# A state-space block's second pass: the sums over states moved from VectorE to ScalarE and accumulating DMAs, with four decay buffers

## The reference

```python
x = x + 0.5 * ffn(layernorm(x))            # ternary weights, bias
x = x + mamba(layernorm(x))
x = x + 0.5 * ffn(layernorm(x))

# inside mamba, per token t, with 16 states n for each of 1024 features d:
dA  = exp(dt[t, d] * A[d, n])              # the decay
dBu = dt[t, d] * B[t, n] * u[t, d]
h   = dA * h + dBu                         # a scan over the 4096 tokens
y[t, d] = sum_n h[d, n] * C[t, n]          # the sum over 16 states
y = (y + u * Dskip) * silu(z);  out = y @ W_out.T
```

## Time and profile before

| what | value |
|---|---|
| median of 3 runs | 3009.37 us (3003.62 to 3009.72) |
| the profiled execution's own time | 2999.02 us |
| its span, first to last instruction | 2997.2 us |
| mean granted TensorE clock | 0.911 of full speed |
| DVE busy | 2510.7 us, 84% of the span |
| PE busy | 2453.4 us, 82% |
| ACT busy | 1956.5 us, 65% |
| POOL busy | 1919.4 us, 64% |

### The profile page before, as it was taken

How to read it: one execution, slowest core, us unless ns; L and a number is a source line. 1 busy time by engine, 2 the same in 40 slices (tenths; PEclk the granted TensorE clock), 3 DMA queues, 4 the chain that set the end, 5 groups by cost and what they waited for, 6 DMA issues and landing times.

```text
span 2997.2 us, 42932 instructions
## 1 busy us (share of the span) xinstructions
PE 2453.4 (82%) x12448; PEld 1406.8 (47%) x12448; DVE 2510.7 (84%) x3325; ACT 1956.5 (65%) x3464; POOL 1919.4 (64%) x1705
## 2 busy tenths in 40 slices
PE   3678898889888736788888888888888888898897
PEld 1333344344343314555555555555555555555553
DVE  5566766767766639999999999999999999999991
ACT  2234756765755756677777777777767776777772
POOL 1112222222221128899989989989989989999993
PEclk8688999999998857899999999999999998999999
DMA  5554323323232245352353342352352352443331
GB/s 198 182 197 148 113 100 128 106 100 134 83 123 106 78 161 164 96 130 72 99 132 82 99 132 77 100 135 71 106 131 76 104 121 82 108 112 94 105 71 42
DMA packets 175914, 337.14 MB, mean 112 GB/s; under 512 B 42721, under 2 KB 92129, under 8 KB 175393
## 3 DMA queue, kind: packets, MB, share of 16 engines
q1 hardware_dynamic: 161824, 283.71, 28.3%
q0 software_dynamic: 13824, 50.34, 8.8%
HBM read 174.09 MB, written 109.58 MB: 95 GB/s over the span
## 4 chain that ended last, share of the span: by engine, by line
POOL 24%; DVE 16%; issue 13%; PE 4%; DMA 3%; ACT 1%; POOLq 1%; DVEq 0%; SPq 0%; ACTq 0%
POOL dbu L1051 19%; DVE h L1275 11%; DVE y L1288 4%; DMA y<-y_part 1%; PE p_g L1407 1%; DMA dtu_<-dtu_scratch 1%; PE p_g L1398 1%; PE p_ht L1364 1%; POOL o L1096 1%; POOL y L1071 1%; POOL carry L1062 1%; POOL x L1090 1%; POOL dbu L1056 1%; POOL y L1086 1%; DMA dt_<-dt_scratch 1%
## 5 line engine op out<-in xcount | busy, mean ns | idle before, releaser
L1275 DVE TENSOR_TENSOR_SCAN h<-p_da,dbu 128x512 f32<-128x512 f32 x1024 | 1188.3, 1205 | 42.6 <-ACT p_da L1157 21.8
L1051 POOL TENSOR_TENSOR dbu<-dtu_,bb 128x1024 f32<-128x1024 f32 x512 | 1203.9, 2380 | 4.6 <-DMA dtu_<-dtu_scratch 4.0
L1157 ACT ACTIVATE p_da<-dt_,neg_a 128x255 f32<-128x255 f32 x2048 | 885.6, 467 | 396.4 <-DVE h L1275 376.0
L1364 PE MATMUL p_ht<-ident,h 128*128 128x128 f32 x4096 | 595.2, 305 | 151.7 <-DVE h L1275 150.3
L1364 PEld LDWEIGHTS p_ht<-ident,h 128*128 128x128 f32 x4096 | 533.5, 159 | 242.6 <-issue 106.6
L1288 DVE SCALAR_TENSOR_TENSOR y<-p_ht,ct,y 128x1024 f32<-128x1024 f32 x400 | 505.5, 1264 | 3.1 <-PE p_ht L1364 3.0
L359 POOL TENSOR_TENSOR late<-dt,u 128x512 f32<-128x512 f32 x64 | 82.3, 1286 | 425.6 <-DVE dt L552 425.6
L1398 PE MATMUL p_g<-wo,tokt 128*128 128x512 f16 x1536 | 352.5, 387 | 1.6 <-ACT tokt L1189 1.6
L710 PE MATMUL p_u<-xz,wu 128*128 128x512 f16 x1536 | 350.0, 385 | 0.0
L1407 PE MATMUL p_g<-wz,xz 128*128 128x512 f16 x1536 | 345.7, 382 | 0.0
L70 POOL TENSOR_TENSOR small<-small,consts 128x1 f32<-128x1 f32 x96 | 70.4, 733 | 404.3 <-DVE small L63 404.3
(11 more groups left out here) (121 smaller groups left out, 3082.0 us busy)
## 6 DMA issues: line engine op xcount, KB each, us to landing
y<-y_part POOLq DMA_DIRECT2D x96, 512.0 KB, 5.8
bb<-b_scratch SPq DMA_DIRECT2D x128, 256.0 KB, 3.5
xin<-in_x SPq DMA_DIRECT2D x32, 512.0 KB, 4.3
x_scratch<-x SPq DMA_DIRECT2D x32, 512.0 KB, 3.3
xz_scratch<-xz SPq DMA_DIRECT2D x16, 1024.0 KB, 6.4
y_scratch<-late SPq DMA_DIRECT2D x32, 512.0 KB, 2.9
dt_scratch<-dt SPq DMA_DIRECT2D x64, 256.0 KB, 2.2
dtu_scratch<-late SPq DMA_DIRECT2D x64, 256.0 KB, 2.5
```

The costliest lines, as they stand in the source:

```text
L1051: nc.gpsimd.tensor_tensor(state[:, 4 * f:4 * f + 4, :], dtu[:, 4 * f:4 * f + 4, :], bb[n // NB % 2][:, n % NB:n % NB + 1, :].to_broadcast( ...
L1157: ins_ = nc.scalar.activation(p_da[p % 2][:, k * T2 + 1:(k + 1) * T2], dt[:, g, 1:], ACT.Exp, scale=neg_a[:, g, n:n + 1])
L1275: nc.vector.tensor_tensor_scan(h[n % 2][:, 2 * p:2 * p + 2, :].rearrange("p g t -> p (g t)"), p_da[p % 2][:], dbu[n % 2][:, 2 * p:2 * p + ...
L1364: mm = nc.tensor.transpose(p_ht[t][:, g * P:(g + 1) * P], h[n % 2][:, g, t * P:(t + 1) * P], ident[:])
```

## The change

1. For t = 1, fifteen states (1 to 15) are now multiplied by ACT; DVE adds only state 0. State 2 goes straight into the single tile `y2`; the other fourteen go through one of three `part` tiles and an accumulating DMA each, in two chains: the odd ones into y itself, the even ones into `y2`. `merge` is an accumulating DMA of y2 into y as well, and stands in the odd chain ahead of state 15. The small POOL instruction ahead of each DMA is gone. Each DMA of a chain waits on POOL until the one before it in the chain has landed.
2. The half bias is added to x1 by an accumulating DMA from a copy in DRAM, which the first pass writes once; and the last sum is one DVE instruction, o = p_g * scale + x1, in place of ACT's L1211 and POOL's L1096.
3. The decays have four buffers, one for each pair: the two PSUM banks for pairs 0 and 1, and two new SBUF tiles `s_da` for pairs 2 and 3.
4. Both passes are written out: no hardware loop is left.
5. The gate of t = 1, the mean and the scale that follow it move one step later, some stores and `add_bias` move earlier.

```diff
-            for j in range(TT1):
-                step(1, 1, j, True, True, True)
-            with eng.Fori(0, (C1 - 4) // 2) as turn:
-                for o in range(2):
-                    for j in range(TT1):
-                        step(turn * 2 + 2 + o, o, j, True, True, True)
-            for j in range(TT1):
-                step(C1 - 2, C1 % 2, j, True, True, True)
+            for i in range(1, C1 - 1):
+                for j in range(TT1):
+                    step(i, i % 2, j, True, True, True)
...
+                    if isinstance(k, int) and k == 2:
+                        sp.wait_ge(const_done, 1)
+                        sp.dma_start(dram["hb"], half_bias[:]).then_inc(hb_stored, 16)
...
+        s_da = [sb(f"s_da{i}", [P, HALF]) for i in range(2)]
...
-        y2 = [sb(f"y2_{i}", [P, D]) for i in range(2)]
-        part = [sb(f"y2_part{i}", [P, D]) for i in range(2)]
+        y2 = sb("y2", [P, D])
+        part = [sb(f"y_part{i}", [P, D]) for i in range(3)]
...
-        p_da = banks("p_da", 2)
+        da = [t[:] for t in banks("p_da", 2) + s_da]
...
-        PARTED = (0, 5, 7, 8, 10, 11, 12)
-        SUMS = len(PARTED) - 1
+        PARTED = tuple(range(1, NS))
+        Y2_FIRST, MERGE = 2, NS
+        Y_SUM, Y2_SUM = (1, 3, 5, 7, 9, 11, 13, MERGE, 15), (4, 6, 8, 10, 12, 14)
+        SUMMED = tuple(n for n in PARTED if n != Y2_FIRST)
+
+        def summed(c, n):
+
+            if n in Y_SUM:
+                return y_summed[c % 2], (c // 2 * len(Y_SUM) + Y_SUM.index(n) + 1) * 16
+            return y2_summed, (c * len(Y2_SUM) + Y2_SUM.index(n) + 1) * 16
+
+        def part_of(c, n):
+
+            return c * len(SUMMED) + SUMMED.index(n)
...
-            body(0, 0)
-            body(1, 1)
-            with eng.Fori(0, (C2 - 4) // 2) as turn:
-                body(turn * 2 + 2, 0)
-                body(turn * 2 + 3, 1)
-            for i in range(C2 - 2, C2 + 2):
+            for i in range(C2 + 2):
                 body(i, i % 2)
...
-                    wait_alone(sp, y_added[1], (c - 1) * NS)
+                    for t in range(TT2):
+                        wait(sp, y_added[t], (c - 1) * NS)
...
-                        if e_on and n in (1, 6, 7):
-                            store(i - 2, *{1: (0, 1), 6: (1, 0), 7: (1, 1)}[n])
+                        if e_on and n in (1, 2, 3):
+                            store(i - 2, *{1: (0, 1), 2: (1, 0), 3: (1, 1)}[n])
...
-                def add_part(c, cpar, k):
-                    wait(pool, y_added[1], c * NS + PARTED[k] + 1)
-                    wait(pool, part_added, (c * SUMS + k - 1) * 16)
-                    nc.gpsimd.tensor_tensor(small[:, 44:45], consts["minus_half"], consts["minus_half"], ALU.mult
-                                            ).then_inc(part_ready, 1)
-                    pool.wait_ge(part_ready, 1)
-                    pool.dma_start(y2[cpar][:], part[k % 2][:], accum_op=ALU.add).then_inc(part_added, 16)
+                def add_part(c, cpar, n):
+                    into, sums, done = (y[cpar][1], Y_SUM, y_summed[cpar]) if n in Y_SUM else (y2, Y2_SUM, y2_summed)
+                    wait(pool, y_added[1], c * NS + n + 1)
+                    if sums.index(n):
+                        wait(pool, *summed(c, sums[sums.index(n) - 1]))
+                    pool.dma_start(into[:], part[part_of(c, n) % 3][:], accum_op=ALU.add).then_inc(done, 16)
 
                 def merge(c, cpar):
-                    wait(pool, y_added[1], c * NS + NS)
-                    wait(pool, part_added, (c + 1) * SUMS * 16)
-                    nc.gpsimd.tensor_tensor(y[cpar][1][:], y[cpar][1][:], y2[cpar][:], ALU.add).then_inc(merged, 1)
+                    wait(pool, *summed(c, Y2_SUM[-1]))
+                    wait(pool, *summed(c, Y_SUM[Y_SUM.index(MERGE) - 1]))
+                    pool.dma_start(y[cpar][1][:], y2[:], accum_op=ALU.add).then_inc(y_summed[cpar], 16)
 
                 def gate(c, cpar, t):
                     wait(pool, y_added[t], c * NS + NS)
                     if t:
-                        wait(pool, merged, c + 1)
+                        wait(pool, *summed(c, Y_SUM[-1]))
...
-                    nc.gpsimd.tensor_tensor(x1[t][:], x1[t][:], half_bias[:], ALU.add).then_inc(xb_done, 1)
-
-                def finish(i, c, t, x):
-                    b, m = place(i, "f", t, x)
-                    wait(pool, g_free[b], m + 1)
-                    wait(pool, xb_done, c * TT2 + t + 1)
-                    nc.gpsimd.tensor_tensor(o[x][:], o[x][:], x1[t][:, x * HALF:(x + 1) * HALF], ALU.add).then_inc(fin_done, 1)
+                    pool.dma_start(x1[t][:], dram["hb"], accum_op=ALU.add).then_inc(xb_done[t], 16)
 
...
-                            if n - 3 in PARTED[1:]:
-                                add_part(i, par, PARTED.index(n - 3))
-                        if e_on:
-                            if n == 1:
-                                finish(i - 1, i - 2, 0, 1)
-                            if n == 5:
-                                add_bias(i - 2, 1)
-                            if n in (6, 7):
-                                finish(i, i - 2, 1, n - 6)
+                            if n - 3 in SUMMED:
+                                add_part(i, par, n - 3)
+                        if e_on and n == 0:
+                            add_bias(i - 2, 1)
                         if c_on:
-                            if n == 3:
+                            if n in (0, 1, 3):
+                                add_part(i - 1, 1 - par, {0: 13, 1: 14, 3: 15}[n])
+                            if n in (2, 5):
+                                gate(i - 1, 1 - par, n // 5)
+                            if n == 2:
                                 merge(i - 1, 1 - par)
-                            if n in (2, 4):
-                                gate(i - 1, 1 - par, n // 4)
                             if n in (10, 13):
                                 row_scale(pool, nc, vn, consts["minus_half"], sn, stats_ready, pow_done, scale_ready,
                                           xn_done, (i - 1) * TT2 + n // 13)
                             if n == 12:
-                                if isinstance(i, int) and i == 1:
-                                    pool.wait_ge(bias_done, 1)
                                 add_bias(i - 1, 0)
-                            if n == 15:
-                                finish(i, i - 1, 0, 0)
...
-                        wait(act, scan_done, i * (NS * 4) + n * 4 + p - 1)
+                        wait(act, scan_done, i * (NS * 4) + n * 4 + p - 3)
                         for k in range(2):
                             g = 2 * p + k
-                            ins_ = nc.scalar.activation(p_da[p % 2][:, k * T2 + 1:(k + 1) * T2], dt[:, g, 1:], ACT.Exp,
+                            ins_ = nc.scalar.activation(da[p][:, k * T2 + 1:(k + 1) * T2], dt[:, g, 1:], ACT.Exp,
...
                 def part_state(i, par, n):
-                    k = PARTED.index(n)
                     if n == PARTED[0]:
                         wait(act, ct_loaded[par], (i - par) * 8 + 16)
-                        wait(act, merged, i - 1)
+                    if n == Y2_FIRST:
+                        into = y2
+                        if i:
+                            wait(act, *summed(i - 1, MERGE))
                     else:
-                        wait(act, part_added, (i * SUMS + k - 2) * 16)
+                        k = part_of(i, n)
+                        into = part[k % 3]
+                        if k >= 3:
+                            wait(act, *summed((k - 3) // len(SUMMED), SUMMED[(k - 3) % len(SUMMED)]))
                     wait(act, ht_full[1], i * NS + n + 1)
-                    nc.scalar.activation((part[k % 2] if k else y2[par])[:], p_ht[1][:], ACT.Copy, scale=ct[par][:, 1, n:n + 1]
+                    nc.scalar.activation(into[:], p_ht[1][:], ACT.Copy, scale=ct[par][:, 1, n:n + 1]
...
-                        if e_on and n in (1, 2):
-                            ffn_out(i, i - 2, 1, n - 1)
-                        if c_on and n in (14, 15):
-                            ffn_out(i, c, 0, n - 14)
...
+                        if c_on and n == 0:
+                            part_state(i - 1, 1 - par, NS - 1)
                         if c_on:
-                            if n in (2, 4):
-                                mean_abs(i, c, 1 - par, n // 4)
-                            if n in (3, 5):
-                                scale_y(c, 1 - par, n // 5)
+                            if n in (2, 5):
+                                mean_abs(i, c, 1 - par, n // 5)
+                            if n in (3, 6):
+                                scale_y(c, 1 - par, n // 6)
...
-                        nc.vector.tensor_tensor_scan(h[n % 2][:, 2 * p:2 * p + 2, :].rearrange("p g t -> p (g t)"), p_da[p % 2][:],
+                        nc.vector.tensor_tensor_scan(h[n % 2][:, 2 * p:2 * p + 2, :].rearrange("p g t -> p (g t)"), da[p],
```

(45 more changed lines are left out.)

11 lines of the change are left out of this document (4 added, 7 removed).

## The result

The changed kernel takes 3211.5 us in the median (3207.31 to 3214.15), the kernel before 3008.61: the ratio is 1.0675, with a 95% interval of 1.0658 to 1.0692. It is slower by 203 us; 312 were forecast.

What follows compares the result with a forecast made beforehand. DVE was taken to bound the second pass. A chunk of 132 us with turn-taking, against 112.5, times 16 chunks gave +312 us: 3311 profiled, 3321 us in the median, range 3050 to 3490 (about 8 in 10).

Steps and rivals of the forecast that it cites:

- The bound and the lengths: Second pass: DVE bounds it, busy 109.4 of 112.5 us a chunk; POOL needs 105.5 us of its own.
- The four decay buffers: Scans of pairs 2 and 3, both inputs in SBUF, take full turns with POOL's SBUF readers; chance 77%.
- the 132 us a chunk: Forecast chunk time with turn-taking in the second pass, between 125.3 (no overlap) and 138.7 (POOL delayed by every such scan).
- the walk of the plain step: One second-pass step followed through: third scan waits 1.3 us for POOL's products; 7.4 us a step in place of 7.03.
- The least that wasn't: Claim that SBUF scans (37.1 us) and POOL's SBUF readers (88.2 us) cannot overlap, so a chunk takes at least 125.3 us.
- A reading of the step: Earlier trace: while POOL's two products run, to 1633.95, DVE does two scans, a sum, two scans, overlapping freely.
- Sums moved off DVE: Eight sums leave DVE (9.4 us a chunk), the final sum comes (2.9): 102.9 us busy, 106.0 with 3.1 idle.
- Rival (a): The scan does not contend, or POOL and DVE pass each other: 106 us a chunk, 2905 us median; chance 13%.
- The expected marks: `s_da` scans well above 1.2 us, `p_da` scans at 1.2, POOL's products about 3 us, chunk 125 to 139 us.
- POOL: POOL loses 13.7 us a chunk of work and gains 9.8 of DMA issues: 101.6 us in place of 105.5.
- DMAs and waits: 17 accumulating DMAs a chunk in place of 6; their landings are met, merge included: nothing taken.
- The written-out passes: Loop-turn waits go, 0 to 28.7 us, not taken off the forecast; the first pass put at nothing.

Runs made afterwards that it cites:

- e1: Changed kernel with its decays back in two PSUM buffers, ACT waiting for the scan two pairs before: 2977.1 us, 0.9902 of the kernel before.
- e2: Changed kernel with only pair 3's decay in one SBUF buffer, the other pairs in PSUM: 3073.7 us, 1.0222 of the kernel before.
- e3: Changed kernel with the decays of all four pairs in two alternating SBUF buffers: 3804.4 us, 1.2645 of the kernel before.
- e7: Kernel before with one of its two decay buffers (pairs 1 and 3) in SBUF, half bias tile 512 wide: 3425.6 us, ratio 1.1392.
- e12: Changed kernel with decay buffers exchanged: pairs 0 and 1 read from SBUF, pairs 2 and 3 from PSUM: 3446.1 us, 1.1446 of the kernel before.
- e6: Changed kernel with DVE's final sum of the first token tile's second half moved ahead of the state sum of n = 15: 3170.6 us, ratio 1.0541.
- e8: Kernel before with both passes written out, nothing else changed: 2979.8 us, 0.9908 of the kernel before.
- e5: As e1, with DVE's final sum of the first token tile's second half ahead of the state sum of n = 15: 2962.4 us, ratio 0.9857.
- e9: As e5, with ACT's copies of the low halves behind the decays of pairs 0 and 1: 2937.4 us, 0.9761 of the kernel before.
- e11: As e5, with each of the fourteen accumulating DMAs a chunk moving 8 of 1024 columns: 2956.8 us, 0.9826 of the kernel before.

## Why the prediction was right, and where it was off

**The bound and the lengths.** DVE bound the second pass and still does, its waits for the port counted with it. The DVE work was right: 102.9 us a chunk were forecast without contention; e1's stretch gives 186.04/200 x 111.6 = 103.8.

**The four decay buffers.** The step that decided was right: two SBUF inputs make a scan take turns with POOL's SBUF readers. The first pass's L631 and L521 carried over to the scan. e1, e2, e3, e7 and e12 show it: no scan above 1.23 us without such inputs, and more time with each pair that has them. The rule of the Trainium skill (page "SBUF — State Buffer", section "Who interferes with whom"), by which a VectorE instruction with two SBUF inputs contends with a GpSimd instruction that reads SBUF, and the one that comes second waits for the other, holds for the scan; the traces agree with up to 4.5 us for a scan of 1.2. The same section of the Trainium skill frees an instruction with at most one SBUF input only outside VectorE's 2-port modes, an exception that the prediction left out; L559 of the earlier trace rows, whose one tensor input is in SBUF, rose to 1496 ns beside POOL, and the scans with a PSUM input never did.

**The term that was mis-sized** is the 132 us a chunk, "the middle of 125.3 and 138.7". Measured: 126.0, near the lower end. I had three numbers and averaged two of them. The upper one supposes POOL never rests; but POOL waits for DVE at the start of each step (116.3 us ahead of L1072), and the fourth scan is free in 241 of 256 steps. e12 shows that this is the luck of the place: with the first pairs in SBUF the chunk takes 141.3, above both my ends. What was to be had from the rows was the walk of the plain step, which had one scan waiting and one free, as in the common step of the timeline; 16 x 7.4 = 118.4 us, it pointed to the lower end. Against the forecast of +312 us, 2016.5 - 1800 = 216.5 us is what the profile holds; the rest is at the ends. Against e1, the SBUF scans hold 512 x 0.54/16 = 17 us a chunk of waits, and DVE's waits for decays are 1.9 us less.

**The least that wasn't.** "No two of these can overlap: 125.3 us a chunk is the least" failed in e6, at 123.9. Two things are wrong with the sum. Records overlap where one engine hands over to the other: in the first step of the timeline, product, scan, product, scan and small add run from 2040.92 to 2047.61, 6.69 us, where the sum has 2 x 2.378 + 2 x 1.161 + 0.21 = 7.29. The rows said so before: after POOL's sum, L631 took 2.15 us more and not its own 2.35. And the port is not always in use: laid over each other, the records of the `s_da` scans and of POOL's tensor_tensor instructions cover 150.9 of 163.2 us a chunk in e3, 130.4 of 138.9 in e7, 120.1 of 126.0 in the changed kernel and 119.8 of 123.9 in e6. The two errors, each of some 4 to 8%, cancel in three kernels; no run shows that they must.

**A reading of the step.** The prediction has DVE do "two scans, a sum, two scans" while the two products run. In the earlier trace rows the products end at 1633.95 and the second pair starts at 1634.18: only the first pair ran beside them. That scans with a PSUM input don't wait is shown by the earlier trace rows all the same.

**Sums moved off DVE.** 6.5 us of work a chunk were to go and 109.4 - 103.8 = 5.6 did, but in e1 the time hardly moves: e8 to e1, which is parts 1, 2 and 5 of the change together, is 0.9908 to 0.9902, nothing within 0.0024. I had kept DVE's idle time at 3.1 us a chunk; it rose to 14/200 x 111.6 = 7.8 in e1. The step that failed is "it costs nothing, unless ACT is held by a late transpose", with the final sum costed at 2.9 us of DVE's time alone. I priced what the final sum does on DVE, not whom it makes wait: it empties the PSUM bank that the next transposes need. e5 and e9 give back 40 us of this. In the changed kernel the same stall stands (80.3 us; first row: ACT waits for transposes too):

```profile
ACT y_part L1170 <- PE p_ht L1369: 170.9, 133, 2.9
...
DVE h L1265 <- ACT p_da L1153: 80.3, 45, 4.0
```

That e6 gains 41 us, where those waits fell by 53, shows that the port and this stall largely add up. Rival (a)'s 2905 us would not have been reached without contention either; e1, at 2977, is that case. What part of the remaining gap is ACT's load and what POOL's issue of DMAs was not separated.

**The expected marks.** The scans of `s_da` rose as said (1.74 us). POOL's products did not rise to 3 us (2.49), and what they rose is not the port's, as e1 has 2.49 too: the one that waits is mostly the small add behind them.

**POOL.** Its net of -3.9 us a chunk can't be read off in the changed kernel, since its busy time holds waits for the port. In e1 it can: 183.35/200 x 111.6 = 102.3 us busy against 103.8 before, -1.5, with the waits behind DMA issues in it.

**DMAs and waits.** Costed at nothing beside the issue, nearly right: ahead of the parts' issues POOL waited 7.1 us in all for landings (4.3 and 2.8), and e11 puts the traffic at 2 to 17 us.

**The written-out passes.** Bounded by 0 to 28.7 us and not taken off again; e8 gives 27, near the upper end. The first pass, put at nothing, has a part in it: the first scan starts 4.2 us earlier.

The account from 3009 to 3211: written out -27 (e8), sums, DMAs and final sum -3, which is nothing within the noise (e1 against e8), decays in SBUF +232 (changed against e1).
